# The last layer's attention computed on rows of bf16 parts that pass through DRAM, and two layer norms in a row as one scaling

## The reference

```python
x = x + _L1_attn_ref(_layernorm(x), wq, wk, wv)      # causal attention with rotary positions
x = x + _L1_ffn_ref(_layernorm(x), ...)              # begins with a second layer norm of its own

def _L1_ffn_ref(x, ...):                             # B=4, S=256, D=256, H=16 heads of dk=16
    xn = layer_norm(x, g1, b1)
    q, k, v = heads(xn @ Wq), heads(xn @ Wk), heads(xn @ Wv)
    scores = einsum('bhqd,bhkd->bhqk', q, k) / sqrt(dk)
    attn = softmax(scores)                           # 64 pairs of batch and head, each 256 x 256
    o = heads_back(attn @ v) @ Wo
    x = x + o
    xn2 = layer_norm(x, g2, b2)                      # then a gate, top 2 of 8 experts, and their sum
    ...
```

## Time and profile before

| what | value |
|---|---|
| median of three runs (lowest, highest) | 1609.24 us (1606.99, 1612.0) |
| the profiled execution | 1606.47 us, its span 1604.7 us |
| last stage's attention loop: first to last score matmul | 1413.7 to 1527.2 us of the span |
| first matmul of the output projection behind the loop | 1535.1 us |
| TensorE busy over the whole span | 1512.1 us, 94% |
| VectorE, ScalarE, GpSimd busy | 70%, 59%, 19% |

### The profile page before, as it was taken

One profiled execution on the slowest core, in us unless ns is written; L12 is line 12 of the kernel. 1 busy time (PEld: TensorE's weight loads), 2 busy tenths in 40 slices (PEclk: granted clock), 3 DMA queues, 4 the chain that ended last, 5 costly groups with the idle time before them and its releaser, 6 DMA issues.

```text
span 1604.7 us, 29140 instructions
## 1 busy us (share of the span) xinstructions
PE 1512.1 (94%) x11450; PEld 936.7 (58%) x11450; DVE 1120.7 (70%) x2352; ACT 943.0 (59%) x2005; POOL 311.5 (19%) x387
## 2 busy tenths in 40 slices
PE   7699999999999999999999988998899998699998
PEld 4355555455555555554555446776567787377765
DVE  4677777877777776777888446676365557667767
ACT  5367777677777777776777732576354433256531
POOL 3362222222222221222100031020100002201110
PEclk9899999999999999999999999999899999899999
DMA  6855635464543646354533060000201102000000
GB/s 181 170 118 121 117 80 99 97 117 96 104 94 74 129 91 120 81 98 91 100 61 59 1 176 1 1 1 0 73 20 47 40 1 80 1 1 1 1 1 27
DMA packets 90169, 111.11 MB, mean 69 GB/s; under 512 B 8048, under 2 KB 82416, under 8 KB 84080
## 3 DMA queue, kind: packets, MB, share of 16 engines
q1 hardware_dynamic: 90032, 109.24, 32.4%
HBM read 81.43 MB, written 27.79 MB: 68 GB/s over the span
## 4 chain that ended last, share of the span: by engine, by line
PE 75%; DVE 9%; ACT 9%; issue 4%; DMA 2%; POOL 1%; SPq 0%; DVEq 0%; ACTq 0%; POOLq 0%
PE psum L511 15%; PE psum L492 12%; PE psum L477 12%; PE psum L265 4%; ACT probs L726 4%; PE psum L2060 3%; PE psum L539 3%; PE psum L1349 3%; PE psum L1629 3%; PE psum L578 3%; PE psum L1611 3%; PE psum L274 2%; PE psum L2108 2%; PE psum L2068 2%; DVE peaks L637 1%
## 5 line engine op out<-in xcount | busy, mean ns | idle before, releaser
L637 DVE TENSOR_REDUCE peaks<-psum 128x1 f32<-128x512 f32 x1024 | 641.5, 684 | 195.5 <-PE psum L477 195.1
L726 ACT ACTIVATE probs<-psum 128x512 f32<-128x512 f32 x1024 | 525.5, 619 | 65.9 <-PE psum L492 62.1
L477 PE MATMUL psum<-keysT,queriesT 96*128 96x512 bf16 x1024 | 389.5, 384 | 13.4 <-DMA keysT<-key_parts 11.8
L492 PE MATMUL psum<-queriesT,keysT 98*128 98x256 bf16 x2048 | 393.6, 274 | 7.8 <-ACT queriesT L785 3.1
L492 PEld LDWEIGHTS psum<-queriesT,keysT 98*128 98x128 bf16 x2048 | 172.4, 99 | 201.7 <-ACT probs L726 82.8
L511 PE MATMUL psum<-probs,values 128*17 128x256 f32 x4096 | 245.9, 381 | 1.1 <-ACT probs L726 1.1
L511 PEld LDWEIGHTS psum<-probs,values 128*17 128x17 f32 x4096 | 107.1, 97 | 103.7 <-issue 26.8
L477 PEld LDWEIGHTS psum<-keysT,queriesT 96*128 96x128 bf16 x1024 | 98.5, 96 | 85.9 <-issue 57.2
L853 POOL CAST key_parts<-key_f 128x512 bf16<-128x512 f32 x59 | 36.2, 614 | 528.3 <-ACT key_f L755 522.9
L755 ACT ACTIVATE key_f<-psum,bk 128x512 f32<-128x512 f32 x59 | 40.5, 687 | 120.0 <-PE psum L539 119.9
L1656 DVE TENSOR_REDUCE peaks<-row_w 128x1 f32<-128x512 f32 x64 | 43.7, 683 | 58.6 <-ACT row_w L1715 58.5
(11 more groups left out here) (251 smaller groups left out, 2014.4 us busy)
## 6 DMA issues: line engine op xcount, KB each, us to landing
key_parts<-key_parts SPq DMA_DIRECT2D x192, 128.0 KB
keysT<-key_parts SPq DMA_DIRECT2D x31, 768.0 KB, 7.7
keysT<-key_parts SPq DMA_DIRECT2D x31, 512.0 KB, 10.1
ctx_nat<-in_ctx_dram SPq DMA_DIRECT2D x32, 256.0 KB, 3.1
keysT<-key_parts SPq DMA_DIRECT2D x31, 256.0 KB, 11.6
ctx_in<-in_ctx_dram SPq DMA_DIRECT2D x24, 256.0 KB, 5.4
q_parts<-q_parts SPq DMA_DIRECT2D x12, 128.0 KB
queriesT<-q_parts SPq DMA_DIRECT2D x8, 192.0 KB, 3.9
```

What stands on the lines that cost most here:

```text
L477: e.matmul(ps, self.queriesT[0:ROWS, u % 2, g * GH + j, t * P:(t + 1) * P], self.keysT[0:ROWS, i % RING, j, c * BANK:(c + 1) * BANK], star ...
L492: made = e.matmul(ps[:, j * S:(j + 1) * S], self.keysT[0:AUG, i % RING, j, kt * P:(kt + 1) * P], self.queriesT[0:AUG, u % 2, g * GH + j, : ...
L637: e.tensor_reduce(self.peaks[:, i % 2, pair, c:c + 1], k.ps(("max", n)), AX.X, ALU.max).then_inc(*self.peaked.up(n))
L726: e.activation(self.probs[:, t % RINGP, e2 * GH * S:(e2 + 1) * GH * S], k.ps(("scores", t, e2)), ACT.Exp).then_inc(*self.exped.up((t, e2)))
```

## The change

1. Where two layer norms follow each other, only the first one's statistics are taken. POOL takes two inverse roots of them for four tiles at once: one for both norms in a row (the variance times 1 + eps, plus eps squared), one for the first norm alone. DVE writes `l.xn` straight from `k.x` with the first; POOL writes `l.x_old` (needed only by the output projection) with the second.
2. The projections of queries and keys are split into three bf16 parts each by a new class `HeadRows`. SP writes them to DRAM and reads them back as 96 rows a head. Two rows of ones for the keys come by DMA from a constant.
3. The loop makes the scores twice in bf16, two groups ahead for the maxima, and has neither the transposes, nor their copies, nor the isolated heads. One exp takes two heads at once (two banks). The scores have banks 0 to 3, the maxima 4 and 5, all else in the loop 6 and 7 in turn.
4. ACT, not DVE, copies the sums of the values. The values have 17 columns a head, not 32 with zeros. Tensors move: the early weights share one tile, which later holds the parts.

The core of the diff:

```diff
+class HeadRows:
+    def first_part(self, e, w, n):
+        w.wait_ge(self.k.projected, self.job(n))
+        e.activation(self.part(n, 0), self.k.ps(self.job(n)), ACT.Copy, scale=self.scale[n % 2])...
+    def rest(self, e, w, n):
+        w.wait_ge(self.part_act, (0, n))
+        ...
+        e.scalar_tensor_tensor(out=self.work[:, n % 2, :], in0=self.k.ps(self.job(n)), scalar=self.scale[n % 2],
+                               in1=self.part(n, 0), op0=ALU.mult, op1=ALU.subtract)...
+    def write(self, e, w, half, m):      # six DMAs of 128 KB
+        for which in range(2):
+            for i in range(PARTS):
+                w.wait_ge(*((self.split, ("part2", n)) if i == 2 else (self.part_act, (i, n))))
+                e.dma_start(self.dram[which, m, :, at, :, own], self.parts[:, which, m, i, own])...
+    def read(self, e, w, m, b0, nb):     # six DMAs: 48, 32 and 16 rows for queries and for keys
+        w.wait_ge(self.written[b0 // 2][m], 0)
+        ...
 class CausalAttention:
     def vector(self, e, w):
-            first.tile(e, w, t)
-            ...
-                second.tile(e, w, u)
+            e.bn_stats(k.stat6[:, t, :], k.x[:, t, :])...
+            e.bn_aggr(k.meanvar[:, t, :], k.stat6[:, t, :])...
             if t == 5:
-                second.scale(e, w)
+                self.norm_twice(e, w, 0)
+            if t % 4 == 3: ... two tensor_scalar of 4 columns
+        self.norm_twice(e, w, 1)
     def gpsimd(self, e, w):
-            norm_inverse(k, e, w, "ffn1 first", half)
-            norm_inverse(k, e, w, "ffn1", half)
+            e.tensor_tensor(both, both, k.constant("minus_half"), ALU.pow)...
+            for i in range(4):
+                e.tensor_scalar(l.x_old[:, u, :], k.x[:, u, :], k.meanvar[:, u, 0:1], l.inverses[:, half, 1, i:i + 1], ...
 class AttentionAndExperts:
     def parts(self):
+        for n in range(4):
+            yield "project", n
+            if n:
+                yield "parts", n - 1
+        yield "parts", 3
+        for t in range(4):
+            yield "v", t
+        yield "turn x", 1
+        for n in range(4, 8):
+            yield "project", n
+            if n > 4:
+                yield "parts", n - 1
+            if n in (5, 6):
+                for h in range(4 * n - 20, 4 * n - 16):
+                    yield "max", h
+        yield "parts", 7
+        for t in range(4, NT):
+            yield "v", t
+        yield "shift", 0
+        for g in range(GROUPS6):
+            for j in range(QUADS):
+                if g + self.AHEAD < GROUPS6:
+                    yield "max", QUADS * (g + self.AHEAD) + j
+                yield "scores", QUADS * g + j
+                if j == 0 and g + 1 < GROUPS6:
+                    yield "shift", g + 1
+                if j == 1 and g >= 2:
+                    yield "gather", g - 2
+                if j == 2 and g >= 1:
+                    yield "values", g - 1
+            ...                              # turn heads, out, norm for batches 0 and 1
     def tensor(self, e, w, banks):
+            elif job == "max":
+                ps = banks.use(4 + n % 2, w, ("max6", n), (self.peaked, n))
+                w.wait_ge(*self.rows.load(h // 8, b))
+                ...                              # two bf16 matmuls, 96 rows, 256 columns
+            elif job == "shift":
+                ps = misc(("shift6", n), (self.shift_kept, n)).bitcast(BF16)
+                w.wait_ge(self.peaked, ("rest", n))
+                ...                              # eight bf16 transposes of 2 columns
+            elif job == "scores":
+                ps = banks.use(n % 4, w, ("scores6", n), (self.exped, n // 2))
+                w.wait_ge(self.shift_kept, n // QUADS)
+                ...                              # two bf16 matmuls, 98 rows, 256 columns
     def scalar(self, e, w):
+            elif job == "shift":                 # 2 x 1024, bf16
+                e.activation(self.rows.rows[0][m][self.ROWS:self.AUG, ...], k.ps(("shift6", n))..., ACT.Copy)...
+            elif job == "scores" and n % 2:      # 128 x 1024, f32
+                e.activation(self.cols_w[:, c0:c0 + 2, :, :]..., k.psum[:, base:base + 2 * BANK], ACT.Exp)...
     def sync(self, e, w):
-        pass
+        self.l.attn1.wait_left(w)
+        ...                                      # two DMAs of ones, 32 KB each
+        for m in range(KD):
+            self.rows.write(e, w, 0, m)
+            self.rows.read(e, w, m, 0, 1)
+        for m in range(KD):
+            self.rows.read(e, w, m, 1, 1)
+        for m in range(KD):
+            self.rows.write(e, w, 1, m)
+            self.rows.read(e, w, m, 2, 2)
```

More of the change, by code:

```diff
@@ L1870, in vector @@
             e.tensor_reduce(self.stat[:, t, 0:1], row, AX.X, ALU.max, negate=True).then_inc(*self.masked.up(("max", t)))
-        first, second = Norm(k, "ffn1 first", k.x, l.x_old), Norm(k, "ffn1", l.x_old, l.xn)
-        done = 0
         for t in range(NT):
+            half = t // 4
             if t % 4 == 0:
@@ L1994, in __init__ @@
         self.mixed, self.summed = sig("mixed"), sig("summed")
-    def heads_ready(self, unit, h):
-        return (self.heads_dve if h % 2 else self.heads_pool), (unit, h)
     def parts(self):
[L2001 to L2021, removed]
-                    yield "norm", 0
[L2023 to L2027, removed]
@@ L2028, in parts @@
+        yield "gather", GROUPS6 - 2
+        yield "values", GROUPS6 - 1
+        yield "turn tokens", 0
+        yield "gather", GROUPS6 - 1
+        yield "turn heads", 2
+        yield "turn heads", 3
         for t in range(4, NT):
@@ L2040, in tensor, with misc @@
         k, l = self.k, self.l
+        turn = 0
+        def misc(job, *let_go):
+            nonlocal turn
+            turn += 1
+            return banks.use(6 + turn % 2, w, job, *let_go)
         wait_half(k, w, "ffn1", 0)
         w.wait_ge(l.w6_in, 0)
[L2043 to L2049, removed]
@@ L2125, in vector @@
         l.attn1.wait_left(w)
-        for name, dst in (("q", self.qT), ("k", self.kT)):
-            for half in range(2):
-                l.keep(e, w, f"{name}6", 2 * half + 1, (f"{name}6", half, 1), dst[:, 1, half * BANK:(half + 1) * BANK],
-                       k.ps((f"{name}6", half, 1)), 1)
-        for t in range(1, NT, 2):
-            self.keep_values(e, w, t, 1)
+        e.tensor_copy(self.ident_b[:, :], k.ident).then_inc(*self.ready.up(0))
         norm = Norm(k, "moe", l.x_old, l.xn)
@@ L2292, in sync @@
     def sync(self, e, w):
-        pass
+        self.l.attn1.wait_left(w)
+        n, first, last = CONST_COLS["ones"]
+        for r in range(self.ROWS, self.AUG):
+            e.dma_start(self.keys[r:r + 1, :, :].rearrange("o h n -> o (h n)").bitcast(F32).rearrange(
+                "o (p n) -> o p n", p=P), self.k.io["const"][:, first:first + H * B * S // 2 // P].unsqueeze(0)).then_inc(
+                *self.ones_in.up(0))
+        for m in range(KD):
[6 more added lines that the diff above has]
+            self.rows.read(e, w, m, 2, 2)
 def build(nc, io, out):
```

297 lines of the change are left out of this document (201 added, 96 removed).

## The result

The changed kernel takes 1568.6 us in the median of four runs (1565.79 to 1570.39), the kernel before 1609.35 (four runs): a ratio of 0.974, interval 0.972 to 0.976. Two more sets of runs gave 1568.18 and 1567.37, with ratios of 0.974 both. The profiled execution took 1570.39 us, its span is 1568.5.

A forecast was written before the change was run, and what follows sets the result against it. TensorE, busy 94% of the span, was taken to bound the kernel. Norms, start-up, loop and tail put the output projection at 1501.1 instead of 1535.1; 34.0 us off 1606.5 gives 1572.5, median near 1575, range 1562 to 1593.

The forecast's parts named there:

- Norms: Layer norms ahead of the attention: one set of statistics lets the first projection start 3.6 us earlier, at 1380.3.
- Start-up: From the first projection to the loop's first scores: these start at 1416, 2.3 us later than before.
- The rows: Query and key parts written to DRAM and read back: landing at 1398.9, just in time for TensorE's first maxima.
- the low clock: Start-up allowance: TensorE's waits lower its clock, adding 1.3 us.
- Loop: The 16 groups of four heads: 4.7 us a group against 6.86 before, 78.6 us in all, ending at 1494.6.
- the wait: In each loop group, TensorE idles 0.7 us for the shift, held by DVE's reduction of the last maxima.
- the mixed-in projection: f32 projection work inside the loop: 4.3 us on TensorE, its statistics pushing DVE by some 1.2 us.
- Tail: From the last scores to the output projection: 6.5 us against 7.9 before.
- A: Rival at the start-up: DRAM writes and reads make the rows late, costing 10 us, 1585; chance 17%.
- B: Rival in the loop: shift, its copy and two shared banks wait in turn, 6.0 us a group, 1593; chance 12%.
- C: Rival in the loop: it runs at TensorE's sum, 4.0 us a group, 10 us less, 1565; chance 16%.
- D: Rival in the loop: the clock falls to 1.2 GHz, 8.5 us a group with the wait, 1637; chance 5%.

The follow-up runs named there:

- e3: The kernel before with only the two layer norms made one scaling; 1602.93 us, ratio 0.9957.
- e5: The changed kernel with the two norms made one after the other, as before the change; 1577.86 us, ratio 0.9813.
- c0_after: The changed kernel run again with nothing altered; 1568.18 us, ratio 0.9743.
- e6: The changed kernel with the previous group's values behind the last scores of a group, not the third; 1568.41 us, ratio 0.9734.
- the controls: Two repeat runs of the changed kernel with nothing altered; 1568.18 and 1567.37 us, ratio 0.9743 both.
- e2: The changed kernel with the norm of batches 0 and 1 and its transposes behind the last two gathers; 1568.16 us, ratio 0.9738.
- e7: e6 with the norm of batches 0 and 1 also moved behind the last gather; 1564.06 us, ratio 0.9713.
- e1: The changed kernel with the next group's shift one head later, behind the second pair of scores; 1582.15 us, ratio 0.9836.
- e8: The changed kernel with all eight of POOL's scalings of x_old put behind both inverse roots; 1571.34 us, ratio 0.9763.
- e9: e8 with the first eight heads' maxima one by one behind the last two projections and four value tiles; 1574.21 us, ratio 0.9776.
- e10: The edits of e9 and e7 together on the changed kernel; 1564.18 us, ratio 0.9722.
- e4: The changed kernel with the first eight heads' maxima spread between the last projections and the value tiles; 1575.19 us, ratio 0.9784.

## Why the prediction was right

The forecast for the profiled run was 1572.5, the span's offset included; it took 1570.39. By the steps:

- *Norms.* First projection forecast 3.6 us earlier, counted from the mark 3.65 to 3.93. The mechanism held. POOL's scalings follow each other 1.36 us apart, DVE's 0.35 to 0.40, and this made a wait that I had not listed (3.1 us on DVE for the second root). The forecast let only the first half of the norms count; e3 and e5 show that the second counts as well.
- *Start-up.* First scores forecast at 1416.0, found at 1417.90, or 2.9 us late when counted from the mark. The rows were right to 0.1 us by the mark (forecast 1398.9, first maximum at 1397.96). Short was the rest: the maxima and the projection between them took 10.0 us, not 8.7 (TensorE waits 1.40 and 2.17 us for maxima behind the remainders in DVE's stream), and the low clock cost more than the 1.3 us that I gave. The last projection and value tiles took 3.78 and 4.67 us here, 3.23 and 3.62 in c0_after, whose first scores come 1.9 us earlier. There the step is 1.0 us off.
- *Loop.* 4.7 us a group forecast, 4.59 found; 3.9 without the wait forecast, 3.94 found in e6; the wait 0.7 forecast, 0.63 found, from the very chain named. The total is the mis-sized term of weight: 78.6 forecast, 71.5 found (1417.90 to the last scores' end at 1489.4). Counted from one group's first scores to the next's, the 7.1 us lie as follows. The first two groups take 3.07 and 3.75 us, not 4.7 each: they have no gather and the first no values (2.6). The next eight take 36.6, not 37.6 (1.0). The five with the mixed-in projection take 5.03, 6.95, 4.79, 4.56 and 4.17 us, 25.5 against 28.6 (3.1): I added this work to the wait, although its matmuls fill it. The last takes 2.5, not 3.0 (0.5). That the wait is filled shows against e6, whose groups have none: the first four of the five are 4.8 us longer there than four plain groups of e6 (20.5 and 15.8), here 3.0 (21.3 and 18.4).
- *Tail.* 6.5 forecast, 9.5 found. The norm's scaling ahead of the divisions, which the forecast put at nothing, is 2.0 of it: counted alike the controls have 8.0, and e2, without the norm there, 6.0. The other 1.5 lie between two runs of the same code, this one with a clock of 0.80 in that stretch, the controls with 1.00, and no run shows what made the clock differ.
- *Balance.* Start +2.9, loop -7.1, tail +3.0, mark -1.0: the projection starts 2.2 us before the forecast's 1501.1. The sum was near because errors of both signs met; each of the three terms was off by about 3 us or more. That it came within 2.1 us of the time is luck. The mechanisms of the norms, the start-up and the loop held, with three gaps: the norms' second half, the filled wait, and the norm in the tail.
- *Rivals.* A (late rows): at most 0.6 to 0.9 us in this kernel; in e5 (3.17 us) and e7 (1.16 us) rows are waited for, once the split comes later or the loop gets there earlier. B: not here, but e1 brings a milder form of it about. C's pace (4.0 us a group) is that of e6, with the values moved. D (clock): the rule of the Trainium skill, "TensorE: Matmul & The Clock Gate", section "A second HAM failure mode: psum-queue depth-cycling", would have the loop swing between the levels. The trace does not agree: the loop idles 0.63 us in each 4.59 and the granted clock stays 1.00. The low level stands where TensorE waits for longer, in the start-up (0.70 from 1400 to 1417, waits of 1.40 and 2.17 us) and behind the loop (0.80 from 1488 to 1495, 2.48 us), but not each time: c0_after has the same wait of 2.48 us behind the loop and a clock of 1.00 (last row):

```profile
1400.00:1417.00 17.00, 14.65 (x46) 7.67 (x46) 9.18 (x18) 3.73 (x8) 0.00 (x0) 0.70 0.99 171
...
1488.00:1495.00 7.00, 4.52 (x42) 2.15 (x42) 3.14 (x12) 2.19 (x4) 1.92 (x2) 0.80 0.00 0
```
```profile
1488.00:1496.00 8.00, 5.05 (x56) 3.09 (x55) 3.81 (x16) 3.79 (x6) 1.93 (x2) 1.00 0.00 0
```

## What to carry to other kernels

Where a value made by another engine returns to TensorE once a group, count what TensorE has to do between the last matmul that feeds it and the first that needs it; moving one independent block of 1 us into that gap was worth 7 us here, moving the consumer instead cost 5 to 6, since it pushed a copy behind an exp and so a bank's release. Work mixed into a loop that waits is not simply added to the wait: in part it fills it. And follow an instruction that is moved on GpSimd to the last small memset behind it.

## What the runs showed of the hardware that I had not expected

- The granted clock in an untouched stretch (1100 to 1180 us) was 0.83, 0.85, 0.87 or 0.94, and carried offsets of up to 7 us into the whole. All three profiles of the changed kernel had 0.94, and so had e5 and e8; e6, e7, e9 and e10, on the same chip as these, had 0.87, and e1 to e4, on another chip, 0.83 to 0.85. Executions of one kernel differ as much in the whole: e6 took 1568.94 us in the profiled one (mean clock 0.976) and 1561.57 in another (0.980). So chance can do it; whether an edit far behind or the chip does too stays open, and so does, for that reason, how much of e6's and e2's gains a median over many runs would show.
- An exp over two banks of PSUM takes 1.02 us for 128 x 1024 elements, and so does the copy of 2 partitions x 1024: the rows' length decides, not their number.

```profile
L2412 ACT ACTIVATE cols_w<-psum 128x1024 f32<-128x1024 f32 x32 | 32.6, 1023 | 2.3 <-PE psum L2232 0.3
...
L2404 ACT ACTIVATE ctx_nat<-psum 2x1024 bf16<-2x1024 bf16 x16 | 16.3, 1016 | 12.1 <-PE psum L2223 12.1
```
